# Later first score chunks at each batch boundary, and expert weights streamed in full through six buffers

## The reference

```
x += tanh(g) * attention_A(norm(x), ctx)     # one head, 1601 context rows, mask added
x += tanh(g) * heads_B(norm(x))              # self attention, 4 of 16 heads picked for each batch
x += tanh(g) * attention_C(norm(x), ctx)     # 16 heads of 16, 1601 context rows, integer mask
x += tanh(g) * experts_D(norm(x))            # each row goes to one of 8 experts by argmax
# experts_D: y = (relu(x @ W1[e] + b1[e]) @ W2[e] + b2[e]) * p,  W1 256 x 1024, W2 1024 x 256
```

## Time and profile before

| | us |
|---|---|
| median of 3 runs | 3057.81 |
| lowest, highest | 3052.07, 3067.73 |
| the profiled execution | 3067.29 |
| its span, first to last instruction | 3065.5 |
| PE busy | 2738.2 (89%) |
| DVE busy | 1742.3 (57%) |
| ACT busy | 1460.1 (48%) |
| POOL busy | 302.8 (10%) |

### The profile page before, as it was taken

How to read it: one execution, slowest core, us unless ns; L and a number is a source line. 1 busy time by engine, 2 the same in 40 slices (tenths; PEclk the granted TensorE clock), 3 DMA queues, 4 the chain that set the end, 5 groups by cost and what they waited for, 6 DMA issues and landing times.

```text
span 3065.5 us, 39733 instructions
## 1 busy us (share of the span) xinstructions
PE 2738.2 (89%) x13624; PEld 1286.6 (42%) x13624; DVE 1742.3 (57%) x4230; ACT 1460.1 (48%) x2922; POOL 302.8 (10%) x352
## 2 busy tenths in 40 slices
PE   5767999899999998999899999999899879968998
PEld 2433343344333433343334333433343323228998
DVE  1336566566666666667666675666666767642111
ACT  2132356544654464546554555455545655632332
POOL 1200010002000200020001000110011000002222
PEclk9878999999999999999999999999999999978999
DMA  4213231323122403231222214231323022046664
GB/s 168 88 32 106 55 96 38 102 49 108 45 84 53 124 17 101 56 102 46 79 78 78 69 39 107 65 87 38 102 57 81 17 60 61 17 135 214 225 216 144
DMA packets 182901, 263.87 MB, mean 86 GB/s; under 512 B 50037, under 2 KB 148573, under 8 KB 182694
## 3 DMA queue, kind: packets, MB, share of 16 engines
q1 hardware_dynamic: 166188, 188.99, 23.3%
q0 software_dynamic: 16512, 72.32, 6.9%
HBM read 200.36 MB, written 60.50 MB: 85 GB/s over the span
## 4 chain that ended last, share of the span: by engine, by line
PE 77%; DVE 9%; issue 5%; ACT 5%; DMA 1%; SPq 1%; POOL 0%; ACTq 0%; POOLq 0%; DVEq 0%
PE PS L1295 13%; PE PS L1251 11%; PE PS L1278 10%; DVE mxC L1752 6%; PE PS L980 6%; PE PS L955 6%; PE PS L1419 5%; PE PS L1430 4%; PE PS L1003 3%; PE PS L1139 3%; PE PS L1048 2%; PE PS L1066 2%; PE PS L1058 2%; ACT reg L878 2%; PE PS L968 2%
## 5 line engine op out<-in xcount | busy, mean ns | idle before, releaser
L878 ACT ACTIVATE reg<-PS 128x512 f32<-128x512 f32 (+1 forms) x1664 | 966.6, 597 | 1073.6 <-PE PS L1278 1067.9
L1752 DVE TENSOR_REDUCE mxC<-PS 128x1 f32<-128x400 f32 (+1 forms) x2048 | 1101.5, 570 | 615.5 <-PE PS L1251 603.0
L1251 PE MATMUL PS<-reg 96*128 96x400 bf16 (+1 forms) x2048 | 670.7, 343 | 98.9 <-DVE mxC L1752 55.5
L1278 PE MATMUL PS<-reg 99*128 99x512 bf16 (+1 forms) x1664 | 618.9, 389 | 38.1 <-ACT reg L878 33.2
L1251 PEld LDWEIGHTS PS<-reg 96*128 96x128 bf16 x2048 | 193.2, 98 | 650.4 <-DVE mxC L1752 479.8
L1295 PE MATMUL PS<-reg 128*17 128x512 f32 (+1 forms) x3328 | 446.1, 609 | 0.0
L1278 PEld LDWEIGHTS PS<-reg 99*128 99x128 bf16 (+1 forms) x1664 | 163.6, 100 | 371.6 <-ACT reg L878 230.0
L955 PE MATMUL PS<-reg 128*128 128x512 f32 (+1 forms) x512 | 219.2, 536 | 6.3 <-issue 4.0
L980 PE MATMUL PS<-reg 128*128 128x512 f32 (+1 forms) x416 | 213.6, 606 | 0.4 <-ACT reg L752 0.4
L901 ACT ACTIVATE reg<-PS,reg 128x128 f32<-128x128 f32 x312 | 89.0, 368 | 215.9 <-PE PS L1419 207.7
L1419 PEld LDWEIGHTS PS<-reg 128*128 128x128 f32 x1248 | 147.7, 194 | 3.1 <-issue 1.0
(11 more groups left out here) (214 smaller groups left out, 2567.1 us busy)
## 6 DMA issues: line engine op xcount, KB each, us to landing
reg<-in_D_W SPq DMA_DIRECT2D x47, 1024.0 KB, 5.6
reg<-in_A_mask POOLq DMA_DIRECT2D x32, 800.5 KB, 5.3
dramK<-reg SPq DMA_DIRECT2D x144, 100.0 KB
dramV<-reg SPq DMA_DIRECT2D x48, 272.0 KB, 2.1
reg<-in_ctxT POOLq DMA_DIRECT2D x8, 1601.0 KB, 9.9
reg<-in_ctx POOLq DMA_DIRECT2D x8, 1536.0 KB, 7.7
dramQ<-reg SPq DMA_DIRECT2D x96, 128.0 KB
reg<-dramQ SPq DMA_DIRECT2D x32, 384.0 KB, 6.5
```

Of the source, the lines that this page charges most:

```text
L878: act.activation(pr[u % RING][0:r, :], PS[0:r, s_bank(v), :], ACT.Exp).then_inc(a_expC, 1)
L1251: last = mm(PS[:, bank, 0:w], qs[(NG * bb + g) % 3][0:ROWS, h, t * P:(t + 1) * P], ks[g % 2][0:ROWS, h, c0:c0 + w], start=True, stop=True)
L1278: last = mm(PS[0:r, bank, :], ks[g % 2][0:STK, h, c * P:c * P + r], qs[(NG * b + g) % 3][0:STK, h, :], start=True, stop=not with_mask)
L1752: v.tensor_reduce(mxC[:, h, t, j:j + 1], PS[:, m_ring(bb, g)[i % len(m_ring(bb, g))], 0:M_CH[j][1]], AX.X, ALU.max).then_inc(v_mx, 1)
```

## The change

Two things are changed.

The first is one row of a table, `PIECES[3]`. The six chunks of steps w = 8, 9 and 10 are taken away there, so that the first chunk is now in step w = 11. The steps 11, 14, 23, 26, 40 and 43 hold one chunk more each. The last chunks are in step 44 as before, and the sum is 64 as before. The row is used at all eight starts of a batch, b = -1 to 6.

The second is the expert stage. W2 is no longer loaded at once and held. `load_weights(j)` now loads W1, b1, W2 and b2 of the tile's expert, W1 and b1 under one semaphore and W2 and b2 under another, and there are six buffers of everything in place of four; load j waits until tile j - 6 is done. PE reads W2 from the tile's buffer at a fixed address, and the loads of PE registers from `tex` are gone, as is the wait for the eight W2 matrices on PE and on SP. PE waits for W2 before `outputs(j)` and DVE before `rows_out(j)`.

```
-WB = 4
+WB = 6
-          "0000000022222213311121322213311121221122111220000000")
+          "0000000000032223311121332223311121221122211320000000")
...
-        w2 = take([NE, FM, D], F32)
...
+        w2 = [take([FM, D], F32) for _ in range(WB)]
...
-                if b == B and u == 6:
-                    sp.wait_ge(pe_pv, UN * B)
-                    for i in range(NE):
-                        sp.dma_start(w2[:, i, :, :], a["D_W2"][i].rearrange("(k p) n -> p k n", p=P)
-                                     ).then_inc(w2_loaded, 16)
...
                 sp.dma_start(w1[par], a["D_W1"][bass.ds(e, 1)].rearrange("o (k p) f -> p (o k) f", p=P)
-                             ).then_inc(w_loaded[par], 16)
+                             ).then_inc(w1_loaded[par], 16)
...
+                sp.dma_start(w2[par], a["D_W2"][bass.ds(e, 1)].rearrange("o (k p) n -> p (o k) n", p=P)
+                             ).then_inc(w2_loaded[par], 16)
...
-            sp.wait_ge(w2_loaded, 16 * NE)
...
-            pe.wait_ge(v_tex, 1)
-            chosen = []
...
             def outputs(j):
+                pe.wait_ge(w2_loaded[j % WB], 32 * (j // WB + 1))
...
-                        last = mm(PS[:, 6 + (NH * j + t) % 2, 0:D], hT[:, m, t * P:(t + 1) * P],
-                                  w2[:, bass.ds(chosen[j], 1), m, :].rearrange("p o n -> p (o n)"),
+                        last = mm(PS[:, 6 + (NH * j + t) % 2, 0:D], hT[:, m, t * P:(t + 1) * P], w2[j % WB][:, m, :],
...
-            pe.wait_ge(w2_loaded, 16 * NE)
             turn_rows(0)
...
                 past(dve, ys_stored[par], 16 * NH * (j // 2))
+                dve.wait_ge(w2_loaded[j % WB], 32 * (j // WB + 1))
```

More of the change, by code:

```diff
@@ L312, in flamingo @@
         take = carve(regC, R - R_AB)
-        w2 = take([NE, FM, D], F32)
-        assert NE * FM * D <= 2 * GH * C + 3 * GH * S // 2 + RING * S + CT * S // 2
-        w1 = [take([KD, FF], F32) for _ in range(WB)]
         hT = take([FM, TS], F32)
         ys = [take([NH, D], F32) for _ in range(2)]
+        w1 = [take([KD, FF], F32) for _ in range(WB)]
+        w2 = [take([FM, D], F32) for _ in range(WB)]
         b1 = [take([FM], F32) for _ in range(WB)]
@@ L366, in flamingo @@
             sem(n) for n in ("g_late", "v_oh", "pe_rank", "v_tex", "v_ohr", "v_oht", "pe_id", "v_id"))
-        w_loaded = [sem(f"w_loaded{i}") for i in range(WB)]
-        w2_loaded = sem("w2_loaded")
+        w1_loaded, w2_loaded = ([sem(f"w{k}_loaded{i}") for i in range(WB)] for k in (1, 2))
         xs_loaded = [sem(f"xs_loaded{i}") for i in range(XB)]
@@ L896, in hidden @@
                 par = j % WB
-                act.wait_ge(w_loaded[par], 48 * (j // WB + 1))
+                act.wait_ge(w1_loaded[par], 32 * (j // WB + 1))
                 for m in range(FM):
@@ L1413, in hidden @@
             def hidden(j):
-                pe.wait_ge(w_loaded[j % WB], 48 * (j // WB + 1))
+                pe.wait_ge(w1_loaded[j % WB], 32 * (j // WB + 1))
                 pe.wait_ge(v_xsT, j + 1)
```

## The result

The changed kernel takes **3040.11 us** (median of 16 runs, 3031.16 to 3051.14) against 3057.93 us for the kernel before (16 runs). The ratio is 0.9934 with a 95% interval from 0.9922 to 0.9946, so it is faster by 0.66%, some 20 us (17.8 between the two medians). The forecast was 3028 with a range from 3014 to 3056. The direction and the range hold, and the saving is about two thirds of the 30 us forecast. The profiled execution took 3039.37 us, against 3067.3 for the profiled one of before, which is a difference of 27.9.

What follows compares the result with a forecast made beforehand. PE's queue was taken as the bound. Stalls 20.5 + clock 15 - given back 6 + first boundary 1 + last 1.8 = 32 us, less 2 for the gather, 30 saved: 3028 us from the 3057.8 median, range 3014 to 3056.

Steps and rivals of the forecast that it cites:

- The bound and the stall: Batch starts: PE's queue is the path; its 31.2 us of waits at the first chunks are for the query reload.
- The middle stalls: Boundaries before batches 1 to 6: moved work fills 3.4 us of each 4.1 us mean stall, saving 20.5 us.
- The half clock: Behind the six middle stalls: 33.6 us at half clock, 0.45 of it won back, 15 us saved.
- Given back: Fuller steps at the six middle boundaries: new waits of chunk matmuls for DVE cost 1.0 us each, 6 us.
- The first boundary: Boundary b = -1: stalls only 1.14 us with no attention beside it; 1 us saved.
- The last boundary and the start of the loop: Before batch 7: 1.8 us saved, 4.8 us stall and low clock stay; tile 0's gather loses 2 us.
- The second part: Expert stage: early W2 loads worth 0; traffic takes 7.1 us per tile, PE stays the bound at 7.26.
- (b): Expert loop turns DMA-bound at 7.8 us per tile, so 13 us saved, 3045 us; chance 0.15.
- (c): Expert loop: mixed queues run well below their single rates, 8.7 us per tile, total 3078 us, slower; chance 0.08.
- where it tips: Expert loop: the traffic may take 7.41 us per tile, some 7.35 less the last landing, before DMAs delay the end.
- (d): Batch boundaries: the query load lands later, the stall stays as long, first part saves 0, 3060 us; chance 0.07.
- (a): Batch boundaries: remaining 0.7 us wait still drops the clock, fuller steps cost 10 us; 11 us saved, 3047; chance 0.13.

Runs made afterwards that it cites:

- e5: The kernel before with the first chunk moved one step later (w = 9) instead of three, expert stage unchanged: 3057.36 us, ratio 1.0005.
- e3: The kernel before with 20 extra matmuls on PE in front of the first chunk's wait, not at the first boundary: 3049.44 us, ratio 0.9967.
- e6: The kernel before, unedited, profiled a second time: 3057.64 us.
- e2: The changed kernel with the old row of chunks, so only the expert stage is changed: 3058.81 us, ratio 1.0001.
- e9: The changed kernel with the old row at the first boundary, a later row for batch 7, and tile 1's weights held until tile 0's gather lands: 3026.22 us.
- e10: e9 with four PSUM banks in place of two for batch 7's first head group: 3026.49 us, ratio 0.9889.
- e1: The kernel before with only the new row of chunks, expert stage as it was: 3037.63 us, ratio 0.993.
- e11: The changed kernel with four buffers for the expert weights in place of six: 3041.67 us, ratio 0.9949.
- e8: The changed kernel with one more 1 MB matrix loaded per expert tile into two buffers nothing reads: 3118.98 us in one run.
- e4: The changed kernel with the first chunk two steps later still (w = 13 in place of 11): 3039.97 us, ratio 0.9934.

## Why the prediction was right in direction and too large

**The bound and the stall.** Right. PE's queue was the path, and the wait at L1251 was for the reload of the queries. It lands when it did: in the interval of batch 2 the first chunk starts 23.4 us behind the projection before (890.88 - 867.45) and 23.6 after (885.63 - 862.07). The work that was moved in front fits in between.

**The middle stalls.** Right. 20.5 us were forecast and the waits of the first chunk fell by 20.6 in the six intervals. e5 adds what the prediction blurred: the three steps do not contribute alike. The forecast's 3.4 us per stall counted ACT's time as filling; PE's own work is 3 x 0.2 + 1.72 + 0.44 = 2.8 us, and the rest is the 0.47 us in which it waits for the exponential. That rest is part of what is given back.

**The half clock.** This is the step that failed most. "Work done at half speed takes half as long at full speed; some of the stretch hangs on DVE, whose speed does not change. I take 0.45 of it, 15 us." e3 gives about 10 us, and the same work in three traces 0.26 to 0.38 of the time at half clock. The half clock itself was there as forecast (33.6 us forecast behind the six stalls, 30.8 gone between e6 and e3). What was mis-sized is its price, 0.45 where 0.30 was measured, and the error is 5 us. The share that hangs on another engine is larger than I took it. The rows of e3 and of the kernel before show it as DVE, which empties the two banks of maxima at its own pace up to the fifth chunk; a kernel with a faster or a slower reduction there was not tried.

**Given back.** Right in size, 6 us forecast, 5.3 measured, and in kind only in part. It was looked for at the chunks (waits for DVE: 0.8 us more) and lies mostly at the score matmul's wait for ACT (3.2 more). The last 1.3 us are not traced. With the clock's 9.2 us (e6 to e3) the sum is 20.6 + 9.2 - 5.3 = 24.5, against the 23.9 between e6 and after. The first and the last term are the measured fall in idle time by construction; what is tested is that e3's 9.2 stands for the 8.6 us by which PE's busy time fell.

**The first boundary.** Wrong in sign: a gain of 1 us was forecast. With the old row there the first interval is 305.7 and 302.9 us in the kernel before, 305.5 in e2, 302.0 in e3, 302.6 in e9 and 305.3 in e10, 304.0 in the mean. With the new row it is 306.5 in after and in e1, 306.8 in e11 and 306.3 in e8, and 309.7 in e4, which starts later still. The cost is 2.5 us. The queries' load is not late there, as the first chunk has no wait. The fourth chunk has one, for DVE, and DVE itself stands before block A's piece L1487, which needs the mask's load:

```profile
263.18 0.69 DVE L1487 CUSTOM_DVE_ANT_0 reg<-PS,reg 128x512 f32<-128x512 f32 x1 [1.89 <-DMA reg<-in_A_mask]
...
264.43 0.34 PE L1245 MATMUL PS<-reg 96*128 96x400 bf16 x1 [2.73 <-DVE mxC L1738]
```

In DVE's queue one reduction now stands ahead of that piece, where the old row has seven, and the six moved ones stand behind it. The wait for the mask shows at this boundary in all five kernels that start at w = 11 or later (1.05 to 1.89 us, and 6.07 in e4) and in none that starts earlier. The prediction did not look at DVE's queue there.

**The last boundary and the start of the loop.** The stall of batch 7 was forecast at 4.8 us and is 5.62, with the low clock behind it (0.74). The gather was forecast to lose 2 us and loses 2.6, of which 1.5 are left at the end of the kernel: from its issue on it is 300.1 us before and 301.6 after. That part is shown by all profiles. It is 300.1 to 300.2 us in the four with W2 loaded at once and 300.0 to 300.1 in e9 and e10, which hold tile 1's weights back, against 301.6 to 303.1 in the five others with the streaming that has no third matrix. e9's stall shrinks from 5.62 to 1.15 us; how much of its 6.4 us ahead of the gather is owed to that is less sure, since this stretch differs by several us between profiles of kernels with the same row.

**The sum.** With 15 replaced by 9 or 10 and +1 by -2.5, the sum of 30 becomes some 21, which is what the timed runs show (20 by the ratio, 21 for e1). That the two profiled executions differ by 27.9 does not speak for the 30. The profiled execution before lay 9.6 us above that of e6, 4.7 of them in the six intervals. Taking the saving from the median was right, and the forecast of 3028 lies below 3040 for the terms named.

**The second part.** Right, but for one reading. W2's early loads were worth nothing (e2), a tile's traffic costs 7.07 us (forecast 7.1), PE stays the bound at 7.26, and the rate is 375 GB/s (forecast 360). Rivals (b) and (c) asked for 7.8 and 8.7 us per tile and are refuted. The price by the busy share, 7.8, was too high, as the forecast took it; that waits of packets for each other are the reason was not tested. Adding single prices holds beyond the tip too, as e8 shows: 7.1 + 2.5 was expected and 9.65 measured. The reading that was wrong is where it tips: the row at 3045.46 is the last tile but one. The trace has PE's first matmul with the last tile's W2 at 3052.34, which leaves (3052.34 - 2771.38) / 37 = 7.59 us per tile and not 7.41. Rival (b) would then have cost some 8 us, not 17. The buffers' number does not matter (e11), as the prediction says of six. Rival (d) falls with the timeline of after, and (a), the clock that stays low behind a short wait, is refuted for the six boundaries of the changed kernel, though e9 has it at batch 7 behind 1.15 us. The forecast's own signs came: no wait over 2 us at batches 1 to 6, a clock of 1.00 behind, tiles at 7.26 us, and for the batch interval that holds the boundary before batch 2, 313.85 us where it was 320.64.

**What stays open.** Executions of one kernel differ by 16 us (the 16 of the kernel before) to 23 us (the 6 of e9). Part of it is the granted clock in the first 540 us, where the kernels do the same work but for the first boundary: PEclk is 0.90 in e2's profile and 0.93 in e3's. The first interval with the old row shows it: by the clock's record PE is at half clock for 30.7 us in the three profiles near 305.5 us (before, e2, e10) and for 23.9 in the three near 302.5 (e6, e3, e9). What sets it was not tried. e9's three edits were not timed one by one, so the timed gain of e9 and e10 over the change is theirs together.

## What to carry to other kernels

Price a stall that is to be filled by the engine's own work in the moved instructions, matmul start to matmul start, and check by adding them up whether the stall goes nearly to zero. Moving a step that holds almost no work of that engine left stall and low clock as they were. Take the value of a clock drop from the same instructions at both levels in the trace, since beside an engine with its own pace it is well below half. When work is moved in one engine's queue, look at what it comes to stand behind in the queues of the others. A table shared by all batches should be read at the first and the last boundary apart from the middle ones, because other work lies beside them: their own rows and the held-back matrix brought some 10 us more by the ratios (0.9934 to 0.9901, and 0.9889 with four banks).

## What the runs showed of the hardware

- A half-clock drop of 6.8 us cost 2.6 us and one of 3.4 us cost 0.87, in the same work. Twenty extra matmuls, 3.55 us together, in each stall kept the clock at 1.00 behind all six boundaries, though up to 1.53 us of wait followed them. Behind batch 7's longer stall, with 3.77 us of wait left, they did not (0.66). In e9 the clock fell there behind a wait of 1.15 us, in a stretch where PE was busy 7.67 us of ten (2440 to 2450).
- Two DMA queues with mixed rows kept 375 GB/s beside a fully busy PE for 100 us, and 384 GB/s when they were the bound, more than W2's loads alone had shown (349).
- The gather of tile 0's rows takes 6.12 us behind the queued weights of tile 1 and 3.43 when they are held back until it has landed. Holding them cost nothing that shows: from the gather's issue to the end it is 300.1 us, as before the change.
